# Gated layers with a routed expert matrix: whole-tile copies on ScalarE, the shift on GpSimd, and weight pieces loaded in pairs

## The chip, the cores and the metric

The kernel is one program on one core of a Trainium2 chip (trn2), written directly against the engines: TensorE (PE, and PEld for its weight loads), VectorE (DVE), ScalarE (ACT), GpSimd (POOL) and SyncE (SP), each with its own list of instructions, synchronised by semaphores. The metric is the device time of one execution in microseconds (us). Several executions of the same kernel are timed; their median is compared.

## What is computed

Inputs are `x` (4 x 1024 x 1024, float32), a context `ctx_512` (4 x 1024 x 256), two gate scalars, and the weights of 8 experts (`W`, 8 x 1024 x 1024, with bias and a router `wg`). Cut to what matters:

```python
# layer 1: a rank-one score plane mixed with the normalised x
si, sj = ctx @ Wi, ctx @ Wj                                  # per token
y  = 0.6 * sigmoid(si[:, :, None] + sj[:, None, :] + b) + 0.4 * layernorm(x)
x1 = x + tanh(g_xattn) * y
# layer 2: each token goes to the one expert with the largest logit
xn = layernorm(x1)
logits = xn @ wg ; probs = softmax(logits) ; idx = argmax(probs)
ffn = probs[idx] * (xn @ W[idx].T + b[idx])
out = x1 + tanh(g_ffn) * ffn
```

The 4096 tokens are handled as 32 tiles of 128 tokens (128 partitions x 1024 values).

## The kernel before

**First stage (32 tiles).** SP loads a tile of x into one of 16 buffers (`xr`). DVE takes its statistics (L773, L778). ACT computes the sigmoid as a tanh of a broadcast row plus a per-token bias (`half_tanh`, L592, three tiles ahead) and gets the sum of the tanh over the row as a by-product. From this sum and the mean ACT computes one number per token, the shift `ln_b` (`shift`, L600). POOL applies scale and shift to the tile (`linear`, L475), DVE adds the tanh (`add_tanh`, L784); this also removes the mean of the new row. PE transposes the tile in eight blocks into PSUM (`turn_tile`, L1060). The transposed tile is copied to SBUF in two halves, the lower by ACT (`copy_turned`, L615) and the upper by DVE (L793); PE multiplies it with the router (`route`, L1073). ACT squares the tile and sums (`square`, L606). Every four tiles DVE chooses experts from the logits (`choose`) and computes each token's place in a table (`position`), and POOL stores the rows of a tile, some six tiles behind, by indirect DMA into a table in DRAM sorted by expert (`store`, L483). SP may load tile t + 16 into a buffer only when the rows of tile t have landed in the table (L342). In the same stage eight groups of context are transposed and multiplied by PE (L1032, L1048), up to about tile 17.

**Second stage (up to 42 slots of 128 rows of one expert, here 36 with work).** A loop of 7 turns of 6 slots runs on each engine; every engine reads for each slot from a table whether there is work, and what kind. A slot's rows are loaded twice: as `xb`, in 32 x 32 blocks so that DVE can transpose them (L858), and as `rows` for the result. The transposed rows are cut into a high part (ACT, L668) and a low part (DVE, L862), and PE does 48 matmuls of 128x512 (L1148; high x high, high x low, low x high). DVE finishes the slot (L872), POOL stores it (L537). Each expert's weights, 8 pieces of 128 output rows, are loaded by SP into a ring of 4 piece buffers (`w_raw`), transposed by DVE (L845), and cut by ACT (L662) and DVE (L850) while PE multiplies with the expert before. Pieces 0 to 3 of the next expert are turned in one slot, pieces 4 to 7 in the next.

**The order on SP** in a slot: wait until the rows two slots ahead are transposed, load `xb` three slots ahead (4 DMAs, L281), wait for the output store of the slot before (L380), load `rows` two slots ahead (L285), then the weight pieces that are due: pieces 0 to 3 of the expert after the next one (L387 to L389), or pieces 4 to 7 of the next (L399 to L401). A piece is four DMAs of 128 KB, one for each quarter of the partitions (`load_piece`, L328 to L332), and each waits until the piece that was in its buffer has been transposed. DVE in a slot turns the rows, then the pieces, then finishes the slot.

PE's wait that matters in the second stage is `pe.wait_ge(finished, t + 1)` (L1143): slot t may begin when slot t - 2 has been finished by DVE.

## Time and profile before

| | us |
|---|---|
| median of 3 runs | 660.69 |
| lowest and highest run | 654.01, 662.92 |
| the profiled execution | 661.08 |
| its span, first to last instruction | 659.4 |
| mean granted TensorE clock, share of full speed | 0.922 |

All times within a trace are us from the start of the span. The views of the trace used below are: windows (busy time of each engine in a stretch, with the granted clock and the share and rate of the DMA engines), groups (instructions of one line, engine and operation; after the bar their busy time in us and the mean of one in ns, then the engine's idle time just before them and what ended it), timelines (instructions of one engine in order of time, equal neighbours merged, with the idle time before them in brackets), and the view of one source line. "issue" as an ender is time for which the trace shows nothing that was waited for. SPq is SP's sequencer, which issues DMAs; the number behind it is the time of the issue, not of the transfer.

### The profile page before, as it was taken

What the parts mean: (1) busy time and instruction counts of PE and PEld (TensorE: products, weight loads), DVE (VectorE), ACT (ScalarE), POOL (GpSimd) and SP (SyncE); (2) the same over time, 40 slices, a digit from 0 to 9 for tenths busy, and PEclk for the clock granted to TensorE, in tenths of its full rate; (3) what the DMA queues carried; (4) which work ended last, traced back from release to release, by engine and by line L of the source; (5) the groups of instructions that cost most, each with busy time, mean ns of one, the idle gap of its engine ahead of it and who ended that gap; (6) DMA issues with size and microseconds to landing.
All of it is one profiled execution on the core that took longest, in us unless ns stands there. A gap on an engine that the chain in (4) does not pass through costs nothing.

```text
span 659.4 us, 14149 instructions
## 1 busy us (share of the span) xinstructions
PE 580.0 (88%) x2877; PEld 461.8 (70%) x2878; DVE 424.7 (64%) x558; ACT 277.1 (42%) x440; POOL 309.7 (47%) x465
## 2 busy tenths in 40 slices
PE   8799988887669999998889999986999899899990
PEld 7677766665428878776668877874887688688870
DVE  4578788786789948825853883775378358834420
ACT  4687677575324424413432441433244224422220
POOL 1356666776412364354345335434353364465640
PEclk9699898699798999998889998987999799999995
DMA  7863766784799875866786687476748575656540
GB/s 259 320 222 105 245 231 257 257 257 163 240 284 241 230 229 189 231 181 213 224 236 183 184 231 242 138 226 193 208 149 249 177 222 163 199 159 196 192 132 14
DMA packets 84537, 136.36 MB, mean 207 GB/s; under 512 B 12048, under 2 KB 64784, under 8 KB 84368
## 3 DMA queue, kind: packets, MB, share of 16 engines
q1 hardware_dynamic: 74576, 101.06, 52.1%
q0 software_dynamic: 9792, 33.82, 13.3%
q14 instruction: 157, 1.29, 0.7%
q8 instruction: 12, 0.20, 0.1%
HBM read 101.01 MB, written 35.93 MB: 208 GB/s over the span
## 4 chain that ended last, share of the span: by engine, by line
SPq 23%; issue 21%; PE 19%; DMA 15%; DVE 9%; POOL 6%; ACT 2%; POOLq 1%; ACTq 1%; DVEq 1%
SPq L330 10%; PE pair L1148 10%; DMA out_x<-rows,scatter_row 5%; PE pair L1073 4%; SPq L281 3%; DMA rows<-table 3%; PE pair L1060 3%; SPq L355 3%; DVE wt L850 2%; DVE xr L784 2%; DMA xb<-table 2%; DMA table<-xr,pos 2%; POOL table L483 2%; POOL xr L475 1%; DVE pair L845 1%
## 5 line engine op out<-in xcount | busy, mean ns | idle before, releaser
L1148 PE MATMUL pair<-wt,xt 128*128 x1728 | 415.6, 404 | 34.4 <-DVE rows L872 28.4
L1148 PEld LDWEIGHTS pair<-wt,xt 128*128 128x128 f32 x1728 | 335.7, 195 | 114.4 <-issue 39.6
L525 POOL TENSOR_TENSOR rows<-rows,rb 128x1024 f32<-128x1024 f32 x37 | 88.8, 2400 | 64.6 <-ACT rb L681 63.0
L858 DVE STREAM_TRANSPOSE pair<-xb 128x1024 f32<-128x1024 f32 x38 | 47.8, 1259 | 97.4 <-DMA xb<-table 65.5
L662 ACT ACTIVATE wt<-pair 128x1024 f32 (+1 forms) x64 | 65.6, 1026 | 80.3 <-DVE pair L845 77.9
L668 ACT ACTIVATE xt<-pair 128x1024 fp32r<-128x1024 f32 x38 | 39.0, 1025 | 118.7 <-DVE pair L858 110.6
L845 DVE STREAM_TRANSPOSE pair<-w_raw 128x1024 f32<-128x1024 f32 x64 | 79.8, 1251 | 4.3 <-DMA w_raw<-in_L_ffn_W 1.9
L850 DVE TENSOR_TENSOR wt<-pair,wt 128x1024 f32 (+1 forms) x64 | 77.3, 1208 | 5.9 <-ACT wt L662 5.9
L518 POOL TENSOR_TENSOR scal<-scal,minus_one 128x1 f32<-128x1 f32 x37 | 20.3, 549 | 116.2 <-ACT ez L673 116.2
L681 ACT ACTIVATE rb<-bias_bc,scal 128x1024 f32 (+1 forms) x37 | 46.0, 1244 | 66.1 <-POOL scal L522 66.1
L1073 PE MATMUL pair<-xc_tr,wg_sb 128*8 128x128 f32 x512 | 68.8, 294 | 0.0
L862 DVE TENSOR_TENSOR xt<-pair,xt 128x1024 fp32r<-128x1024 f32 x38 | 46.5, 1223 | 32.9 <-ACT xt L668 28.6
L475 POOL TENSOR_SCALAR xr<-xr,ln_a,ln_b 128x1024 f32<-128x1024 f32 x32 | 45.2, 1414 | 41.4 <-ACT ln_b L600 40.1
L872 DVE SCALAR_TENSOR_TENSOR rows<-pair,scal,rows 128x1024 f32<-128x1024 f32 x36 | 46.1, 1280 | 21.3 <-PE pair L1148 21.3
L1073 PEld LDWEIGHTS pair<-xc_tr,wg_sb 128*8 128x8 f32 x512 | 46.8, 96 | 16.1 <-issue 3.0
L1060 PE MATMUL pair<-ident,xr 128*128 128x128 f32 x256 | 38.3, 297 | 16.4 <-DVE xr L784 16.0
L1060 PEld LDWEIGHTS pair<-ident,xr 128*128 128x128 f32 x256 | 30.9, 153 | 23.5 <-DVE xr L784 21.7
L606 ACT ACTIVATE th<-xr 128x1024 f32<-128x1024 f32 x32 | 33.7, 1052 | 27.6 <-DVE xr L784 27.3
L483 POOL DMA_INDIRECT table<-xr,pos x32 | 35.4, 1105 | 21.0 <-DVE pos L822 11.1
L784 DVE SCALAR_TENSOR_TENSOR xr<-th,c,xr 128x1024 f32<-128x1024 f32 x32 | 42.0, 1312 | 3.4 <-POOL xr L475 3.4
L537 POOL DMA_INDIRECT out_x<-rows,scatter_row x36 | 38.6, 1072 | 11.7 <-issue 6.6
L773 DVE BATCH_NORM_STATS2 raw<-xr 128x6 f32<-128x512 f32 x64 | 40.7, 678 | 3.7 <-DMA xr<-in_x 3.7
(128 smaller groups left out, 384.3 us busy)
## 6 DMA issues: line engine op xcount, KB each, us to landing
w_raw<-in_L_ffn_W SPq DMA_DIRECT2D x256, 128.0 KB
xb<-table SPq DMA_DIRECT2D x156, 128.0 KB
rows<-table SPq DMA_DIRECT2D x38, 520.0 KB, 3.7
xr<-in_x SPq DMA_DIRECT2D x32, 512.0 KB, 6.3
ctx_in<-in_ctx SPq DMA_DIRECT2D x8, 512.0 KB, 5.8
bias_bc<-in_L_ffn_b SPq DMA_DIRECT2D x8, 512.0 KB
sj<-sj_row SPq DMA_DIRECT2D x3, 512.0 KB
out_x<-rows,scatter_row POOLq DMA_INDIRECT x36, 4.6
```

What stands on the lines that cost most here:

```text
L330: sp.dma_start(w_raw[32 * q:32 * (q + 1), m % WR, :, :], in_blocks(W[bass.ds(e, 1), P * m:P * (m + 1), :].rearrange("a o h -> (a o) h"), q ...
L475: nc.gpsimd.tensor_scalar(xr[:, s, 0:H], xr[:, s, 0:H], ln_a[:, t:t + 1], ln_b[:, t:t + 1], ALU.mult, ALU.add).then_inc(lin_ready, 1)
L483: nc.gpsimd.indirect_dma_start(out=table, out_offset=bass.IndirectOffsetOnAxis(ap=pos[:, t:t + 1], axis=0), in_=xr[:, s, :], in_offset=Non ...
L525: nc.gpsimd.tensor_tensor(rows[:, k, 0:H], rows[:, k, 0:H], rb[:, :], ALU.add).then_inc(base_ready, 1)
L662: nc.scalar.activation(wt[:, bass.ds(par, 1), 0, :, P * m:P * (m + 1)].rearrange("p a k o -> p (a k) o"), ps[:, :].rearrange("p (k o) -> p ...
L784: nc.vector.scalar_tensor_tensor(out=xr[:, s, 0:H], in0=th[:, t % RTH, :], scalar=c2[:, 0:1], in1=xr[:, s, 0:H], op0=ALU.mult, op1=ALU.add ...
L845: nc.vector.transpose(turned(ps), blocked(w_raw[:, m % WR, :, :])).then_inc(w_turned, 1)
L850: nc.vector.tensor_tensor(where[:, :, 1].rearrange("p a k o -> p (a k) o"), ps[:, :].rearrange("p (k o) -> p k o", k=K), where[:, :, 0].re ...
L858: nc.vector.transpose(turned(ps), blocked(xb[:, k, :, :])).then_inc(xb_turned, 1)
L1060: last = nc.tensor.transpose(xt_ps[t % 2][:, P * k:P * (k + 1)], xr[:, slot_of(t), P * k:P * (k + 1)], ident[:, :])
L1073: last = nc.tensor.matmul(lgt_ps[:, r, :], wg_sb[:, k, :], xc_tr[:, t % 2, k, :], start=(k == 0), stop=(k == K - 1))
L1148: last = nc.tensor.matmul(out_ps[r % 2][:, HALF * h:HALF * (h + 1)], xt[:, r % RING, x_part, k, :], wt[:, bass.ds(par, 1), w_part, k, HALF ...
```

## The change

1. `shift` moves from ACT to POOL, directly ahead of `linear` of the same tile.
2. The copy of a transposed tile is one instruction of 128x1024 on ACT; DVE's half is gone. PE signals once for all eight blocks.
3. ACT's order within a tile: square of the tile before, copy of this tile, tanh of three tiles ahead (before: tanh of three tiles ahead, square of this tile, copy, shift).
4. Weight pieces load two to a transfer: four DMAs of 256 KB for a pair instead of eight of 128 KB. A pair waits until both pieces in its buffers are transposed, and has one semaphore.
5. POOL looks at the first slot of a turn and, if it has no work, passes the whole turn.

```diff
-            def load_piece(e, m):
+            def load_pieces(e, m):
                 for q in (0, 2, 1, 3):
-                    sp.dma_start(w_raw[32 * q:32 * (q + 1), m % WR, :, :],
-                                 in_blocks(W[bass.ds(e, 1), P * m:P * (m + 1), :].rearrange("a o h -> (a o) h"),
-                                           q)).then_inc(w_landed[m % WR], 16)
+                    sp.dma_start(w_raw[32 * q:32 * (q + 1), m % WR:m % WR + 2, :, :].rearrange("i a b c -> i (a b) c"),
+                                 W[bass.ds(e, 1), P * m:P * (m + 2), QW * q:QW * (q + 1)]
+                                 .rearrange("a (b i) c -> i (a b) c", i=32)).then_inc(w_landed[m % WR // 2], 16)
...
-                                for m in range(WR, K):
-                                    sp.wait_ge(w_turned, K * e + K + m - WR + 1)
-                                    load_piece(e + 1, m)
+                                for m in range(WR, K, 2):
+                                    sp.wait_ge(w_turned, K * e + K + m - WR + 2)
+                                    load_pieces(e + 1, m)
...
+            def shift(t):
+                pool.wait_ge(th_ready, t + 1)
+                pool.wait_ge(ln_ma_ready, t // GR + 1)
+                nc.gpsimd.tensor_scalar(ln_b[:, t:t + 1], xr[:, slot_of(t), TH:TH + 1], nc2h[:, 0:1],
+                                        ln_ma[:, t:t + 1], ALU.mult, ALU.add).then_inc(ln_b_ready, 1)
...
                 if t + 2 < T:
+                    shift(t + 2)
                     linear(t + 2)
...
+                with pool.If(pool.value_load(slot_tab[0:1, 0, bass.ds(TURN * i, 1)], min_val=0, max_val=4) > 0):
+                    slot(TURN * i, 0, i)
+                    for r in range(1, TURN):
...
+                with pool.Else():
+                    pool.nop()
...
-                nc.scalar.activation(xc_tr[:, t % 2, 0:K // 2, :].rearrange("p k n -> p (k n)"),
-                                     xt_ps[t % 2][:, 0:HALF], ACT.Copy).then_inc(xc_copied[0], 1)
+                nc.scalar.activation(xc_tr[:, t % 2, :, :].rearrange("p k n -> p (k n)"), xt_ps[t % 2][:, :],
+                                     ACT.Copy).then_inc(xc_copied, 1)
...
-                if t + RTH - 1 < T:
-                    half_tanh(t + RTH - 1)
-                square(t)
-                copy_turned(t)
-                if t + 2 < T:
-                    shift(t + 2)
+                if t:
+                    square(t - 1)
+                copy_turned(t)
+                if t + RTH - 1 < T:
+                    half_tanh(t + RTH - 1)
...
-            def copy_turned(t):
-                dve.wait_ge(xc_turned[1], t + 1)
...
-                nc.vector.tensor_copy(xc_tr[:, t % 2, K // 2:K, :].rearrange("p k n -> p (k n)"),
-                                      xt_ps[t % 2][:, HALF:2 * HALF]).then_inc(xc_copied[1], 1)
...
-                dve.wait_ge(w_landed[m % WR], 128 * e + 64 * (m // WR) + 64)
+                dve.wait_ge(w_landed[m % WR // 2], 128 * e + 64 * (m // WR) + 64)
```

The program of ACT in the first stage, tile 6 of the kernel before. L592 is the tanh of tile 9, L606 the square of tile 6, L615 the copy of its lower half, L600 the shift of tile 8; the next row begins tile 7.

```order
L592 ACTIVATE th,xr<-sj,si_half 128x1024 [waits xc_ready,mv_ready,sq_ready,si_ready,sj_landed]
L606 ACTIVATE th,xr<-xr 128x1024 [waits xc_ready]
L615 ACTIVATE xc_tr<-pair0 128x512 [waits routed,xc_turned0]
L600 ACTIVATE ln_b<-xr,ln_ma,nc2h 128x1 [waits ln_ma_ready,th_ready]
L592 ACTIVATE th,xr<-sj,si_half 128x1024 [waits xc_ready,mv_ready,sq_ready,si_ready,sj_landed]
```

The same engine and tile in the changed kernel, with its own line numbers: L618 is the square of tile 5, L627 the copy of the whole of tile 6, L611 the tanh of tile 9, and the next row the square of tile 6.

```order
L618 ACTIVATE th,xr<-xr 128x1024 [waits xc_ready]
L627 ACTIVATE xc_tr<-pair 128x1024 [waits routed,xc_turned]
L611 ACTIVATE th,xr<-sj,si_half 128x1024 [waits xc_ready,mv_ready,sq_ready,si_ready,sj_landed]
L618 ACTIVATE th,xr<-xr 128x1024 [waits xc_ready]
L627 ACTIVATE xc_tr<-pair 128x1024 [waits routed,xc_turned]
```

The tanh has moved from ahead of the square to behind the copy, the shift has left the engine, and the copy is twice as wide.

DVE in the first stage, one tile of the kernel before, from the addition to the next one:

```order
L784 SCALAR_TENSOR_TENSOR xr<-th,c,xr 128x1024 [waits lin_ready]
L773 BN_STATS raw<-xr 128x6 [waits x_landed9]
L773 BN_STATS raw<-xr 128x6
L793 COPY xc_tr<-pair 128x512 [waits routed,xc_turned1]
L778 BN_AGGR xr<-raw 128x2 [waits raw_ready]
```

And of the changed kernel:

```order
L794 SCALAR_TENSOR_TENSOR xr<-th,c,xr 128x1024 [waits lin_ready]
L783 BN_STATS raw<-xr 128x6 [waits x_landed9]
L783 BN_STATS raw<-xr 128x6
L788 BN_AGGR xr<-raw 128x2 [waits raw_ready]
L794 SCALAR_TENSOR_TENSOR xr<-th,c,xr 128x1024 [waits lin_ready]
```

The copy and its wait for PE have gone; nothing that DVE waits for within a tile comes from PE any more, save for the choice of experts once in four tiles.

SP in the second stage, the end of a second half in the kernel before (the last piece of an expert; `ISA` rows compute an address):

```order
L400 REGISTER_ALU
L330 ISA [waits w_turned]
L330 DMA w_raw<-in_L_ffn_W 32x4x256
L330 ISA
L330 DMA w_raw<-in_L_ffn_W 32x4x256
...
```

And in the changed kernel (the second pair):

```order
L401 REGISTER_ALU
L331 ISA [waits w_turned]
L331 DMA w_raw<-in_L_ffn_W 32x8x256
L331 ISA
L331 DMA w_raw<-in_L_ffn_W 32x8x256
...
```

Before, this piece of program with one wait and four DMAs stands four times in a half expert, now twice, each DMA with eight blocks of 1 KB for a partition instead of four.

## Rows read from the trace of the kernel before

**Rows 1.** Windows: stretch, length, busy us of each engine, PEclk, DMA share, GB/s.

```profile
42.00:83.00 41.00, 40.36 (x306) 32.20 (x307) 33.83 (x67) 32.32 (x66) 24.45 (x28) 0.88 0.46 157
83.00:166.00 83.00, 67.48 (x527) 52.91 (x528) 63.79 (x124) 54.90 (x113) 57.09 (x61) 0.92 0.66 230
...
198.00:642.00 444.00, 415.55 (x1728) 335.62 (x1728) 276.19 (x265) 154.88 (x205) 204.38 (x327) 0.96 0.68 201
...
230.00:241.00 11.00, 9.42 (x42) 7.43 (x41) 6.96 (x8) 3.48 (x7) 6.54 (x12) 1.00 0.84 264
...
397.00:403.00 6.00, 6.00 (x21) 4.75 (x21) 3.58 (x4) 1.42 (x3) 4.74 (x9) 0.76 0.82 239
```

**Rows 2.** Groups of the first stage, from 83 to 166 us.

```profile
L475 POOL TENSOR_SCALAR xr<-xr,ln_a,ln_b 128x1024 f32<-128x1024 f32 x18 | 26.2, 1454 | 14.4 <-ACT ln_b L600 13.4 <-issue 0.5
...
L1060 PE MATMUL pair<-ident,xr 128*128 128x128 f32 x148 | 22.0, 296 | 15.5 <-DVE xr L784 15.2 <-issue 0.2
...
L773 DVE BATCH_NORM_STATS2 raw<-xr 128x6 f32<-128x512 f32 x25 | 16.0, 680 | 2.3 <-DMA xr<-in_x 2.3
L793 DVE COPY xc_tr<-pair 128x512 f32<-128x512 f32 x18 | 12.4, 689 | 11.3 <-PE pair L1060 10.9 <-issue 0.5
L615 ACT ACTIVATE xc_tr<-pair 128x512 f32<-128x512 f32 x18 | 10.4, 578 | 1.1 <-PE pair L1060 1.0
L600 ACT ACTIVATE ln_b<-xr,ln_ma,nc2h 128x1 f32<-128x1 f32 x17 | 6.4, 375 | 2.4 <-POOL ln_ma L469 2.4
```

**Rows 3.** Groups of the second stage, from 198 to 642 us.

```profile
L1148 PE MATMUL pair<-wt,xt 128*128 x1728 | 415.6, 404 | 34.4 <-DVE rows L872 28.4 <-DVE xt L862 5.9
...
L845 DVE STREAM_TRANSPOSE pair<-w_raw 128x1024 f32<-128x1024 f32 x57 | 71.4, 1253 | 4.3 <-DMA w_raw<-in_L_ffn_W 1.9 <-issue 0.7
L850 DVE TENSOR_TENSOR wt<-pair,wt 128x1024 f32 (+1 forms) x58 | 70.0, 1206 | 3.1 <-ACT wt L662 3.1
...
L858 DVE STREAM_TRANSPOSE pair<-xb 128x1024 f32<-128x1024 f32 x37 | 46.6, 1259 | 96.0 <-DMA xb<-table 64.2 <-issue 31.7 <-DVE xt L862 0.2
```

**Rows 4.** Timeline of PE, slots 7 and 8 together and slot 9.

```profile
281.52 22.61 PE L1148 MATMUL pair<-wt,xt 128*128 x96 [2.71 <-DVE rows L872]
306.55 12.86 PE L1148 MATMUL pair<-wt,xt 128*128 x48 [2.41 <-DVE rows L872]
```

**Rows 5.** Timeline of SP: start, time of the issues, number.

```profile
280.06 9.49 SPq L330 DMA_DIRECT2D w_raw<-in_L_ffn_W  x16
296.03 1.82 SPq L281 DMA_DIRECT2D xb<-table  x4
...
316.73 8.48 SPq L330 DMA_DIRECT2D w_raw<-in_L_ffn_W  x16
```

**Rows 6.** Timeline of DVE in the same stretch.

```profile
287.52 1.26 DVE L858 STREAM_TRANSPOSE pair<-xb 128x1024 f32<-128x1024 f32 x1 [6.41 <-issue]
...
301.25 1.26 DVE L858 STREAM_TRANSPOSE pair<-xb 128x1024 f32<-128x1024 f32 x1 [8.84 <-DMA xb<-table]
...
322.40 1.26 DVE L845 STREAM_TRANSPOSE pair<-w_raw 128x1024 f32<-128x1024 f32 x1
...
325.99 1.26 DVE L845 STREAM_TRANSPOSE pair<-w_raw 128x1024 f32<-128x1024 f32 x1 [1.22 <-DMA w_raw<-in_L_ffn_W]
```

**Rows 7.** Groups with like work: a small one on POOL (stage two), a whole-tile copy on ACT (0 to 30 us).

```profile
L510 POOL TENSOR_SCALAR scal<-rows,c2h,c 128x1 f32<-128x1 f32 x36 | 12.3, 341 | 3.6
...
L565 ACT ACTIVATE xc_tr<-pair 128x1024 f32<-128x1024 f32 x2 | 2.0, 1024 | 0.3 <-PE pair L1032 0.3
```

**Rows 8.** SP's first issues: the timeline, and the source line L300 (ns min/median/max).

```profile
2.24 0.60 SPq L293 DMA_DIRECT2D gates<-in_g_xattn  x1
...
L300 SPq DMA_DIRECT2D xr<-in_x x4: 443/466/3893, 7.0 to 11.9; - x4
```

**Rows 9.** The ends of POOL and SP: durations in ns, first and last start.

```profile
L66 POOLq DRAIN  x1: 5628/5628/5628, 652.7 to 652.7; - x1
...
L66 SPq DRAIN  x1: 13/13/13, 659.2 to 659.2; - x1
```

More of the change, by code:

```diff
@@ L180, in build @@
         row_stored = [sem(f"row_stored{s}") for s in range(RX)]
-        w_landed = [sem(f"w_landed{s}") for s in range(WR)]
+        w_landed = [sem(f"w_landed{s}") for s in range(WR // 2)]
         xb_landed = [sem(f"xb_landed{s}") for s in range(2)]
@@ L213, in build @@
         sq_ready = sem("sq_ready")
-        xc_turned = [sem(f"xc_turned{h}") for h in range(2)]
-        xc_copied = [sem(f"xc_copied{h}") for h in range(2)]
+        xc_turned = sem("xc_turned")
+        xc_copied = sem("xc_copied")
         routed = sem("routed")
@@ L342, in _ @@
                 sp.dma_start(xr[:, slot_of(t), 0:H], tile_of(x_t, t)).then_inc(x_landed[slot_of(t)], 16)
-            for m in range(WR):
-                load_piece(0, m)
-            for m in range(WR, K):
-                sp.wait_ge(w_turned, m - WR + 1)
-                load_piece(0, m)
+            for m in range(0, WR, 2):
+                load_pieces(0, m)
+            for m in range(WR, K, 2):
+                sp.wait_ge(w_turned, m - WR + 2)
+                load_pieces(0, m)
             for s in range(RX):
@@ L360, in _ @@
             load_blocks(sp, row_of(2), 2)
-            for m in range(WR):
-                sp.wait_ge(w_turned, K - WR + m + 1)
-                load_piece(1, m)
+            for m in range(0, WR, 2):
+                sp.wait_ge(w_turned, K - WR + m + 2)
+                load_pieces(1, m)
             with sp.Fori(0, SLOTS // TURN) as i:
@@ L488, in _ @@
             norm_scalars(0)
-            linear(0)
-            linear(1)
+            for t in range(2):
+                shift(t)
+                linear(t)
             for t in range(T):
@@ L529, in _, with slot @@
             pool.wait_ge(limits_told, 1)
[L530 to L543 removed]
+            def slot(t, r, i):
+                slot_scalars(t + 1, 2 * i + (r + 1) // RING, (r + 1) % RING)
+                settled(finished, t + 3)
+                nc.gpsimd.indirect_dma_start(
+                    out=out_rows,
+                    out_offset=bass.IndirectOffsetOnAxis(ap=scatter_row[:, r % RING:r % RING + 1], axis=0),
+                    in_=rows[:, r % RING, 0:H], in_offset=None,
+                    bounds_check=N - 1, oob_is_err=False).then_inc(out_stored[r % RING], 16)
+            with pool.Fori(0, SLOTS // TURN) as i:
+                with pool.If(pool.value_load(slot_tab[0:1, 0, bass.ds(TURN * i, 1)], min_val=0, max_val=4) > 0):
+                    slot(TURN * i, 0, i)
+                    for r in range(1, TURN):
+                        t = TURN * i + r
+                        work = pool.value_load(slot_tab[0:1, 0, bass.ds(t, 1)], min_val=0, max_val=4)
+                        with pool.If(work > 0):
+                            slot(t, r, i)
+                        with pool.Else():
+                            pool.nop()
+                    pool.nop()
+                with pool.Else():
+                    pool.nop()
             held = [pool.value_load(in_place[0:1, s:s + 1], min_val=1, max_val=SLOTS) for s in range(RING)]
@@ L594, in half_tanh @@
                                      accum_out=xr[:, slot_of(t), TH:TH + 1]).then_inc(th_ready, 1)
-            def shift(t):
-                act.wait_ge(th_ready, t + 1)
-                act.wait_ge(ln_ma_ready, t // GR + 1)
-                nc.scalar.activation(ln_b[:, t:t + 1], xr[:, slot_of(t), TH:TH + 1], ACT.Identity,
-                                     bias=ln_ma[:, t:t + 1], scale=nc2h[:, 0:1]).then_inc(ln_b_ready, 1)
             def square(t):
@@ L875, in _ @@
             turn_weights(0, 0, cut_a, 0)
-            for h in range(2):
-                dve.wait_ge(xc_copied[h], T)
+            dve.wait_ge(xc_copied, T)
             turn_weights(0, 1, pair[1], 1)
@@ L1055, in turn_tile @@
                 if t >= 2:
-                    for h in range(2):
-                        pe.wait_ge(xc_copied[h], t - 1)
-                for h in range(2):
-                    for k in range(K // 2 * h, K // 2 * (h + 1)):
-                        last = nc.tensor.transpose(xt_ps[t % 2][:, P * k:P * (k + 1)],
-                                                   xr[:, slot_of(t), P * k:P * (k + 1)], ident[:, :])
-                    last.then_inc(xc_turned[h], 1)
+                    pe.wait_ge(xc_copied, t - 1)
+                for k in range(K):
+                    last = nc.tensor.transpose(xt_ps[t % 2][:, P * k:P * (k + 1)],
+                                               xr[:, slot_of(t), P * k:P * (k + 1)], ident[:, :])
+                last.then_inc(xc_turned, 1)
             def route(t):
-                for h in range(2):
-                    pe.wait_ge(xc_copied[h], t + 1)
+                pe.wait_ge(xc_copied, t + 1)
                 g, r = t // GR, t % GR
```

32 lines of the change are left out of this document (6 added, 26 removed).

## The prediction

> **What bounds the kernel now.** I read the windows of each stage first, then the groups of instructions of one stage at a time with what ended their idle time, and last the timelines of single engines. The windows [rows 1] show three different limits. From 42 to 83 us PE is busy 40.36 of 41 us: nothing that frees another engine can shorten this stretch by more than 0.6 us. From 83 to 166 us it is busy 67.48 of 83. From 198 to 642 us it is busy 415.55 of 444, the last 17 us of the span have no matmul.
>
> In the stretch 83:166 the 18 linear steps (L475) stand for 18 tiles [rows 2], so a tile takes 83/18 = 4.6 us. Busy time per tile is PE 3.75, DVE 63.79/18 = 3.54, POOL 57.09/18 = 3.17, ACT 54.90/18 = 3.05 [rows 1]. No engine is full; what is left is waiting in a ring: PE waited 15.2 us for the addition on DVE, DVE 10.9 us for PE before its half of the copy, POOL 13.4 us for ACT's shift ln_b [rows 2].
>
> In the second stage the reader is to see that PE's idle time ends with DVE's finish of an earlier slot: 28.4 us in sum [rows 3]. DVE in turn spent 64.2 us waiting for the transfer xb, and 1.9 us for weights. A slot of 48 matmuls at full pace is 22.61/2 = 11.3 us; the one behind the pause of 2.41 us takes 12.86 [rows 4]. The granted clock falls in such a place: 0.76 of the full 2.4 GHz on average in 397:403, behind a pause, against 1.00 in 230:241 [rows 1]. 1728/48 = 36 slots of 11.3 are 407 us, so 444 holds 37 us of pauses and slow starts. That is the most that the second part of the change can touch.
>
> Where does xb come late? On SP. The 16 weight transfers that begin at 280.06 take 9.49 us; the next xb loads are issued at 296.03, though the transpose that frees their buffer began at 287.52 and took 1.26 [rows 5, 6]. DVE then stood 8.84 us until 301.25, and PE paused before 306.55 [rows 4, 6]. There are six such groups in the loop, one for the first four pieces of each of the experts 2 to 7.
>
> **First stage, part by part.** DVE loses its copy: 0.689 us a tile and the 10.9 us of waits with it [rows 2]; its busy time falls to 3.54 - 0.69 = 2.85. ACT gets a whole tile instead of a half: a 128x1024 copy out of PSUM took 1.024 against 0.578 [rows 2, 7], so +0.45, and loses the shift, 0.375: 3.05 + 0.07 = 3.12. POOL gets the shift: its own 128x1 tensor_scalar with two scalar columns took 0.341 [rows 7]; with the wait for its own result I take 0.45 (between 0.34 and 0.8), so 3.62. The 13.4 us for which POOL waited on ACT goes, since tanh of a tile is done two tiles ahead. Square one tile behind costs nothing of itself: the store that reads its sum runs six tiles behind, and the tanh that overwrites the same buffer follows it on ACT anyway; were it waited for, it would be 1.24 a tile. ACT's tanh for three tiles ahead now stands behind the copy, which waits for PE; from its end to the addition that needs it there are shift 0.45, linear 1.45, and two tiles of time, so that wait is not expected to be seen.
>
> Next in line are PE with 3.75 and POOL with 3.62 a tile, both close together, so that neither will run without holes. The floor is 3.75: 18 x (4.6 - 3.75) = 15 us, which is PE's wait again. The other end: POOL's collisions, the store-to-load ring (16 buffers; DVE already waited 2.3 us for x [rows 2]), and no gain or +2. I take 4.2 a tile, a bit under the middle: 18 x 0.4 = **-7 us**, range -14 to +2.
>
> **Second stage.** Half as many issues with twice the descriptors. A transfer of 128 descriptors costs SP 9.49/16 = 0.59 us, or 8.48/16 = 0.53 where nothing presses [rows 5]. 256 descriptors in one transfer are not in the trace. The nearest row is the load of 512 single weights (L292): the issue behind it (L293) took 0.60 us. The load of wg, 1024 pieces of 32 bytes, was followed by an issue of 3.89 us (L300, the longest) [rows 8]; a proportional price from it would be 0.97 for 256. So 0.53 to 1.0; I take 0.6, the nearer row. Eight issues are then 4.8 us for 8.5 to 9.5, and SP is at the next xb 4 us sooner. With 1.0 it is no sooner at all.
> The Trainium skill (DMA: Bandwidth & Descriptors, Anatomy of one DMA) says that many descriptors can be emitted before the incremental cost shows up. By it the issue would stay at 0.53 and the gain be near 4.5 us a group; by the wg row it would be nothing. No row here decides between them.
> The bytes do not get fewer. From 230 to 241 us the DMA engines were 0.84 busy at 264 GB/s [rows 1] while 16 pieces' transfers were on their way, and xb now queues behind them. So I count 3.5 us of the 4 for a group. Six groups make 21 us of earlier xb. Of this PE sees what stands before a pause. Some of DVE's long waits the view puts down to issue, not to xb (6.41 us at 287.52) [rows 6], and DVE's own work stays: eight pieces of 1.253 + 1.206 = 19.7 us and twice some 3.7 for the rows and the finish, 27 us, against the 22.6 of two slots on PE [rows 3, 4]. I take 0.6: -13 us.
>
> The other side of the pair: the first piece of a second half can be turned only when its pair has landed. At 316.73 SP begins to issue; DVE turns that first piece at 322.40 and the second at 325.99, after 1.22 us of waiting [rows 5, 6]. Pairs make the first wait for what the second waited for: 0 to 3.6 us, in seven places. The faster issue takes most of it back; I take 0.3 each, +2. SP's wait for turned pieces asks for one piece more, 2.5 us later on DVE. The queue behind it on SP is the rest of the group and the next xb. But where SP begins the second half, at 316.73, DVE's next weight transpose is already the first of that half, so all four of the first are turned [rows 5, 6]: nothing. Sum of the stage **-11 us**, range -22 to +14.
>
> **The stages between and the end.** Between the last tile and the first slot the pieces that share the queue with the last stores are the same bytes: 0, within 1.5 us. In the last turn all six slots are empty. POOL passes one instead of six, but the span does not end with POOL: its drain began at 652.7 and took 5.6, to 658.3, and SP's came last, at 659.2 [rows 9]. SP skips less code now, so what can be had is some 0.9 us: **-1**, range -1 to 0.
> The Trainium skill (Runtime: NRT & Kernel Launch, Instruction fetch mechanics) says that a taken branch out of the fetched window forces a fetch by DMA. DVE's 6.41 us marked issue at 287.52 [rows 6] fit that. By that rule deeper bursts of weights could lengthen such fetches; it is part of the slow rival.
>
> Sum, from the profiled execution's 661.08 (span 659.4, 1.7 around it; the runs' median is 660.69): 661.1 - 7 - 11 - 1 = 642.
>
> **Rivals.**
> A. Issue time goes with descriptors. Then SP is as late as before and stage two gives 0, the pair still costs 2: 661 - 7 + 2 - 1 = 655. For it the wg row; against it the row of 512.
> B. POOL is the new bound of stage one, as the ring of stores and loads holds it at 4.6 a tile; stage two works: 661 - 11 - 1 = 649.
> C. Everything lands: 661 - 14 - 20 - 1 = 626. For it the regular shape of late xb before each pause; against it the DMA share of 0.84 in a group.
> D. Slower: DVE's first piece of each second half waits for its pair. The place is the transpose L845 behind L858 in the seven second-half slots, the price up to 3.6 us each, and as DVE works through there without a pause all of it reaches PE: 25 us. It decides from the point where a pair needs more than the 322.40 - 316.73 = 5.7 us between SP's first issue and DVE's turn. With the first stage's gain 661 + 25 - 7 = 679. Against it: a pair is 1 MB, some 4 us at 264 GB/s.
> E. The change of POOL's turns does nothing because another engine ends last: this is in the forecast already.
>
> **How the numbers follow.** Forecast 0.44 (634 to 648), A 0.21, B 0.16, C 0.13, D 0.06. A measurement tells about 2%, 13 us. Faster than 647.5: most of the forecast's share, C, and a small part of B: 0.58. Within 2%: A, most of B and the rest: 0.37. Slower: 0.05. The range leaves out the far half of C and all of D: 628 to 659.
>
> **What would show it.** Right: in 83:166-like stretches the additions come every 4.2 us, POOL's wait for ln_b is gone, ACT's copy is 1.02; an issue of a double transfer is 0.4 to 0.5 long; xb is issued 3 us or more sooner behind the six groups; DVE's waits for xb fall from 64 to under 50 us and PE's pauses from 28.4 to under 18. Wrong: an issue near 1 us, DVE waiting for w_raw by over 5 us in sum, POOL busy over 90% in the first stage, or PE's pauses as long as before.

## The result, and the profile after

The changed kernel takes 668.84 us (median of 4 runs, 665.38 to 670.98), the kernel before 657.35 (4 runs, 651.73 to 662.92). The ratio is 1.016, with a 95% interval of 1.011 to 1.021: slower by about 11 us, where 642 had been forecast, and outside the range. The profiled execution of the changed kernel took 669.64 us.

The windows of the changed kernel. The columns are those of [rows 1]. The row 189.20:649.10 holds exactly the 1728 matmuls of the second stage, the last row what follows them.

```profile
span 667.8 us, 13667 instructions
...
core 0: us, PE busy (x) PEld busy (x) DVE busy (x) ACT busy (x) POOL busy (x), PEclk, DMA share, GB/s
83.00:166.00 83.00, 67.28 (x554) 52.56 (x552) 55.40 (x116) 60.67 (x100) 64.89 (x78) 0.95 0.76 255
...
189.20:649.10 459.90, 416.70 (x1728) 337.38 (x1728) 276.79 (x265) 154.50 (x205) 205.10 (x328) 0.94 0.74 194
258.00:271.00 13.00, 13.00 (x59) 10.66 (x58) 9.81 (x10) 5.62 (x7) 5.67 (x9) 1.00 1.04 237
649.10:667.80 18.70, 0.01 (x1) 0.00 (x0) 1.28 (x1) 0.00 (x0) 1.07 (x1) 0.60 0.04 11
```

The kernel before, cut at the same places:

```profile
197.90:642.00 444.10, 415.64 (x1728) 335.72 (x1728) 276.29 (x265) 154.88 (x205) 204.38 (x327) 0.96 0.68 201
642.00:659.40 17.40, 0.00 (x1) 0.00 (x0) 1.28 (x1) 0.00 (x0) 1.07 (x1) 0.61 0.04 13
```

So the second stage began 8.7 us sooner, took 15.8 us longer, and what follows it 1.3 us longer: 659.4 - 8.7 + 15.8 + 1.3 = 667.8. Note the DMA share: 0.74 against 0.68 of the engines' time, for a rate of 194 against 201 GB/s. The same bytes keep the DMA engines busy for longer.

The first stage, groups of the window 83:166 (compare [rows 2]):

```profile
L483 POOL TENSOR_SCALAR xr<-xr,ln_a,ln_b 128x1024 f32<-128x1024 f32 x17 | 25.4, 1493 | 1.7
...
L794 DVE SCALAR_TENSOR_TENSOR xr<-th,c,xr 128x1024 f32<-128x1024 f32 x18 | 23.3, 1297 | 5.7 <-POOL xr L483 5.7
L1057 PE MATMUL pair<-ident,xr 128*128 128x128 f32 x144 | 20.2, 284 | 12.5 <-DVE xr L794 12.5
...
L627 ACT ACTIVATE xc_tr<-pair 128x1024 f32<-128x1024 f32 x18 | 18.3, 1018 | 18.7 <-PE pair L1057 18.7
...
L477 POOL TENSOR_SCALAR ln_b<-xr,nc2h,ln_ma 128x1 f32<-128x1 f32 x16 | 7.2, 448 | 2.7 <-ACT th L611 2.2
```

POOL's 13.4 us of waiting for ln_b became 2.7 us ahead of the shift, the copy takes 1.018, and the shift 0.448 where 0.45 was taken. Counting additions in the window misleads, 18 before and 18 after, because the last tile now ends inside it. By the timeline the 18 additions from 84.67 to 155.35 are 17 tiles in 70.7 us, 4.16 a tile; before they were 4.56.

The second stage, what DVE and PE waited for (compare [rows 3]):

```profile
L1144 PE MATMUL pair<-wt,xt 128*128 x1728 | 416.7, 405 | 50.0 <-DVE rows L872 43.2 <-DVE xt L862 6.8
```

```profile
engine line waited for: us in total, times, longest us
DVE pair L858 <- issue: 52.5, 15, 12.7
DVE xt L862 <- ACT xt L678: 39.6, 27, 3.8
DVE rows L872 <- PE pair L1144: 27.3, 7, 5.6
DVE pair L858 <- DMA xb<-table: 25.8, 10, 6.4
DVE pair L845 <- DMA w_raw<-in_L_ffn_W: 16.3, 11, 3.1
```

Waiting for xb fell from 64.2 to 25.8 us, the way that was forecast. But "issue", time for which the profile names no releaser, rose from 31.7 to 52.5, and waiting for weights from 1.9 to 16.3. PE's pauses behind DVE's finish went from 28.4 to 43.2.

SP's timeline (start and length in us), one group of weights, answers to [rows 5], where 16 transfers took 9.49 us:

```profile
277.10 5.50 SPq L331 DMA_DIRECT2D w_raw<-in_L_ffn_W  x8
292.49 1.83 SPq L281 DMA_DIRECT2D xb<-table  x4
```

Issuing is cheap, as forecast: no group of eight in the second stage takes longer than 6.6 us, waits included. But the xb behind this group was issued 15.4 us after its first transfer, for 16.0 us in [rows 5]. The queues and transfers on the page of the changed kernel:

```profile
q1 hardware_dynamic: 72528, 101.05, 57.6%
...
w_raw<-in_L_ffn_W SPq DMA_DIRECT2D x128, 256.0 KB, 6.5
```

The last number is the median time from issue to landing. A group of eight doubles is issued in 3.9 to 6.6 us, but its last byte lands 12 to 16 us after the first issue, no sooner than that of 16 single transfers (11 to 14 us in the first experiment). The xb that SP issued at 264.90, early, landed from 272.7 to 275.2, behind weights of which the last landed at 270.7. DVE turned it only at 291.89, so this late landing alone cost nothing.

### The profile page after: what moved, and what is told of

It is laid out like the page before. It is cut to its first block, busy times and chain, and to the rows that moved or that the text cites. A ratio compares the mean times of both kernels' runs of the same rounds, so it can differ in the third digit from the quotient of the medians.

```text
span 667.8 us, 13667 instructions
## 1 busy us (share of the span) xinstructions
PE 573.7 (86%) x2877; PEld 457.3 (68%) x2878; DVE 403.9 (60%) x526; ACT 280.3 (42%) x408; POOL 326.6 (49%) x497
## 3 DMA queue, kind: packets, MB, share of 16 engines
q0 software_dynamic: 9792, 33.82, 13.3%
## 4 chain that ended last, share of the span: by engine, by line
DMA 25%; issue 19%; PE 19%; POOL 9%; SPq 9%; DVE 9%; ACT 4%; POOLq 1%; ACTq 1%; DVEq 1%
PE pair L1144 10%; DMA out_x<-rows,scatter_row 9%; DMA w_raw<-in_L_ffn_W 8%; PE pair L1069 4%; DVE wt L850 3%; SPq L331 3%; DMA rows<-table 3%; DVE pair L845 3%; POOL table L491 3%; PE pair L1057 2%; DMA table<-xr,pos 2%; ACT rb L691 2%; SPq L281 2%; POOL xr L483 1%; SPq L356 1%
## 5 line engine op out<-in xcount | busy, mean ns | idle before, releaser
L1144 PE MATMUL pair<-wt,xt 128*128 x1728 | 416.7, 405 | 50.0 <-DVE rows L872 43.2
L858 DVE STREAM_TRANSPOSE pair<-xb 128x1024 f32<-128x1024 f32 x38 | 47.8, 1258 | 80.7 <-issue 52.5
L845 DVE STREAM_TRANSPOSE pair<-w_raw 128x1024 f32<-128x1024 f32 x64 | 80.1, 1254 | 19.0 <-DMA w_raw<-in_L_ffn_W 16.3
L1069 PEld LDWEIGHTS pair<-xc_tr,wg_sb 128*8 128x8 f32 x512 | 46.4, 95 | 15.4 <-issue 3.0
L794 DVE SCALAR_TENSOR_TENSOR xr<-th,c,xr 128x1024 f32<-128x1024 f32 x32 | 41.7, 1302 | 13.4 <-POOL xr L483 13.2
L1057 PE MATMUL pair<-ident,xr 128*128 128x128 f32 x256 | 36.4, 287 | 12.5 <-DVE xr L794 12.5
L491 POOL DMA_INDIRECT table<-xr,pos x32 | 37.5, 1171 | 16.5 <-DVE pos L823 6.4
L483 POOL TENSOR_SCALAR xr<-xr,ln_a,ln_b 128x1024 f32<-128x1024 f32 x32 | 43.4, 1356 | 3.2
L627 ACT ACTIVATE xc_tr<-pair 128x1024 f32<-128x1024 f32 x32 | 32.6, 1017 | 26.3 <-PE pair L1057 26.3
L1057 PEld LDWEIGHTS pair<-ident,xr 128*128 128x128 f32 x256 | 29.8, 149 | 18.9 <-DVE xr L794 16.1
## 6 DMA issues: line engine op xcount, KB each, us to landing
bias_bc<-in_L_ffn_b SPq DMA_DIRECT2D x8, 512.0 KB, 10.4
```

The source lines that it names most:

```text
L483: nc.gpsimd.tensor_scalar(xr[:, s, 0:H], xr[:, s, 0:H], ln_a[:, t:t + 1], ln_b[:, t:t + 1], ALU.mult, ALU.add).then_inc(lin_ready, 1)
L491: nc.gpsimd.indirect_dma_start(out=table, out_offset=bass.IndirectOffsetOnAxis(ap=pos[:, t:t + 1], axis=0), in_=xr[:, s, :], in_offset=Non ...
L845: nc.vector.transpose(turned(ps), blocked(w_raw[:, m % WR, :, :])).then_inc(w_turned, 1)
L858: nc.vector.transpose(turned(ps), blocked(xb[:, k, :, :])).then_inc(xb_turned, 1)
L1057: last = nc.tensor.transpose(xt_ps[t % 2][:, P * k:P * (k + 1)], xr[:, slot_of(t), P * k:P * (k + 1)], ident[:, :])
L1069: last = nc.tensor.matmul(lgt_ps[:, r, :], wg_sb[:, k, :], xc_tr[:, t % 2, k, :], start=(k == 0), stop=(k == K - 1))
```

## Experiments

Ratios are to the kernel before, run in turn on the same chip, with their 95% interval. "First slot", "second stage" and "tail" are the start of the 1728 matmuls, their duration, and the rest of the span, of one profiled execution each; they scatter by some 3 us. The intervals are 0.3 to 0.6 points to either side, so a difference of less than some 0.7 points between two of these ratios is not told apart from noise.

**1. Single pieces again, all else changed** (four transfers of 128 KB with a semaphore and a wait of their own; the other calls alike).

```diff
-                for m in range(0, WR, 2):
-                    load_pieces(e + 2, m)
+                for m in range(WR):
+                    load_piece(e + 2, m)
```

> The changed kernel with its weight pieces loaded one by one again (128 KB transfers, one semaphore and one wait per piece), all else as changed. Theory (the loss is in the paired loads alone): the first slot begins near 189 us as in the changed kernel (before: 197.9), the second stage is back at 444 us instead of 460, and the time is 1.2 to 1.5% below the kernel before, about 649 of 657. DVE waits for weight pieces under 4 us in sum (16.3 in the changed kernel). Rival (the early start of the second stage, or a change elsewhere, spoils its order): the second stage stays over 452 us and the time is at or above the kernel before.

Ratio 0.998 (0.994 to 1.002). First slot 194.5, second stage 445.5, tail 18.9. The loss is in the paired loads, as the theory says; DVE's wait for weights was 2.7 us. But the rest of the change wins almost nothing, where 1.2 to 1.5% was expected.

**2. The kernel before with paired loads alone** (part 4 of the diff, nothing else).

> The kernel before with the paired loads alone. Theory (pairs cost the second stage 16 us by themselves): the first slot begins near 198 us, the second stage takes about 460 us, the time is 2.0 to 2.7% above the kernel before. Rival (the pairs hurt only together with the other parts, as what precedes them has moved): within 1% of the kernel before.

Ratio 1.017 (1.012 to 1.022), first slot 200.8, second stage 457.4. Pairs cost the same by themselves, if a little less than the 2.0 to 2.7% expected. The rival is out.

**3. The pair's wait with 128 KB transfers.**

```diff
-                for q in (0, 2, 1, 3):
-                    sp.dma_start(w_raw[32 * q:32 * (q + 1), m % WR:m % WR + 2, ...
+                for n in (m, m + 1):
+                    for q in (0, 2, 1, 3):
+                        sp.dma_start(w_raw[32 * q:32 * (q + 1), n % WR, ...
```

> The changed kernel, but a pair goes out as eight transfers of 128 KB in the order of the kernel before; the pair's wait on SP and its single semaphore stay. Theory 1 (the price is the wait: the first piece of a pair is turned only when both have landed): as slow as the changed kernel, ratio 1.01 to 1.02, DVE waits for weight pieces over 14 us. Theory 2 (the price is the form of the transfers: twice as long in one quarter of the partitions, at 218 GB/s, and issued in a denser burst): close to the kernel with single pieces, ratio 0.985 to 0.995, waits of DVE for weights under 8 us. Between them: both have a share.

Ratio 0.990 (0.985 to 0.994), second stage 442.1. The wait for the pair costs nothing; the form of the transfers is the loss, 2.6% between this kernel and the changed one. DVE waits for weights 10.4 us, where under 8 was expected, and the kernel is none the slower for it. DVE's waits:

```profile
DVE pair L859 <- issue: 44.0, 14, 9.1
DVE pair L859 <- DMA xb<-table: 38.9, 14, 6.1
DVE xt L863 <- ACT xt L679: 30.3, 25, 2.6
DVE rows L873 <- PE pair L1145: 22.0, 5, 5.6
DVE pair L846 <- DMA w_raw<-in_L_ffn_W: 10.4, 7, 2.3
```

**4. Single pieces, quarters in the order 0, 1, 2, 3** (experiment 1 with another order, nothing else).

> The kernel with single pieces (as the first of these runs), but the four transfers of a piece go to the quarters of the partitions in the order 0, 1, 2, 3 instead of 0, 2, 1, 3, so that two in a row lie in the same half of the partitions, 256 KB as in a double transfer. Theory (the double transfers are slow because both halves' ports are not in use together): the rate in a group of pieces falls from about 260 towards 220 GB/s and the second stage becomes 5 to 15 us longer than with 0, 2, 1, 3. Rival (it is the wait, or the denser issue): the time is within 0.5% of the kernel with single pieces in the order 0, 2, 1, 3.

Ratio 0.996 (0.992 to 0.999). Both are half right: the bytes move more slowly, but here it cost no time. The first pair of rows is of experiment 1, the second of this one:

```profile
q1 hardware_dynamic: 74576, 101.06, 52.2%
...
w_raw<-in_L_ffn_W SPq DMA_DIRECT2D x256, 128.0 KB, 3.3
```

```profile
q1 hardware_dynamic: 74576, 101.06, 56.4%
...
w_raw<-in_L_ffn_W SPq DMA_DIRECT2D x256, 128.0 KB, 3.9
```

Times the spans (658.9 and 652.0), the 101 MB took 344 us of the 16 engines' time in one order and 368 in the other; the doubles took 385.

**5. Doubles with a pause between them**, in the loop alone (`paced` is set there).

```diff
                                 .rearrange("a (b i) c -> i (a b) c", i=32)).then_inc(w_landed[m % WR // 2], 16)
+                    if paced:
+                        sp.value_load(slot_tab[0:1, 0, 0:1], min_val=0, max_val=4)
```

> The changed kernel with its double transfers, but in the loop SP reads one register value (about 0.6 us) behind each of them, so that 256 KB are issued every 1.1 us, as densely as the single pieces were. Theory (the dense burst is what hurts: it fills the queue ahead of xb and of the other transfers): the time comes back to near the kernel with 128 KB transfers and the pair's wait, ratio 0.99 to 1.00. Rival (the size of a transfer and the speed at which it moves is what hurts, however it is spaced): ratio 1.01 to 1.02 as the changed kernel, or worse by the delay.

Ratio 1.010 (1.004 to 1.016). Eight issues took 7.9 to 10.0 us, 16 single ones 7.6 to 9.8 in experiment 1. It lies at the lower end of what the rival expected. Spacing takes back 0.6 of 2.6 points at most, and that is within the noise.

**6. All engines pass an empty turn**, on top of experiment 3; SP, ACT, PE and DVE get what the change gave POOL:

```diff
             with dve.Fori(0, SLOTS // TURN) as i:
+                with dve.If(dve.value_load(slot_tab[0:1, 0, bass.ds(TURN * i, 1)], min_val=0, max_val=4) > 0):
                     for r in range(TURN):
...
+                with dve.Else():
+                    dve.nop()
```

> The kernel with the pair's wait and 128 KB transfers, and SP, ACT, PE and DVE also pass a whole turn when its first slot is empty, as POOL does. Theory (the end is set by DVE and SP, which step through six empty slots at 1.5 to 2.6 us each behind the last matmul): the tail behind the last matmul falls from 18.7 us to 9 to 12, and the time by 6 to 9 us against the same kernel without it, ratio to the kernel before 0.975 to 0.982. Rival (the last transfers or the fetch of the code behind the loop set the end): tail over 16 us, no gain.

Ratio 0.989 (0.984 to 0.995), where 0.975 to 0.982 was expected. The tail did what was expected:

```profile
190.20:639.30 449.10, 413.37 (x1728) 334.76 (x1728) 276.22 (x265) 154.56 (x205) 204.53 (x327) 0.96 0.67 199
639.30:652.10 12.80, 0.00 (x0) 0.00 (x0) 1.28 (x1) 0.00 (x0) 1.07 (x1) 0.64 0.03 11
```

12.8 us instead of 18.7: behind the last matmul it was DVE and SP that stepped through six empty slots. In this execution DVE was done 4.7 us behind the last matmul and POOL's drain came last. In the changed kernel, where only POOL passed the turn, POOL's drain could begin at 6.8 us but DVE came to its own at 18.4. The second stage was 7 us longer than in experiment 3, and ate the gain. Why is open; the code of every engine has moved.

**7. The first stage's edits alone** (parts 1 to 3 on the kernel before).

> The kernel before with the first stage's three edits alone (shift on GpSimd, whole copy on ScalarE, square one tile behind); single pieces, and GpSimd steps through every slot. Theory (they win what the trace showed, 8 to 9 us, and the rest of the kernel keeps its time): ratio 0.985 to 0.990. Rival (the win is partly given back in the second stage, because DVE's program has moved and its taken branches fetch code more often: 33 fetches over 0.35 us instead of 28 in the kernels with these edits): ratio 0.993 to 1.000 and a second stage longer than 444 us.

```profile
188.30:634.30 446.00, 410.85 (x1728) 332.54 (x1728) 276.38 (x265) 154.40 (x205) 204.59 (x327) 0.96 0.68 201
634.30:652.70 18.40, 0.00 (x0) 0.00 (x0) 1.28 (x1) 0.00 (x0) 1.07 (x1) 0.63 0.04 13
```

Ratio 0.999 (0.996 to 1.002): the rival. The first slot begins at 188.3, almost 10 us sooner, but the stage is 2 us and the tail 1 us longer, and the profiled execution was a quick one (654.4 to 662.9, median 658.3).

**8. Doubles in one half of an expert only.** In 8a pieces 0 to 3 go as doubles and 4 to 7 as in experiment 3; in 8b it is the other way round.

> Doubles of 256 KB only for pieces 0 to 3 of each expert (loaded one expert ahead); pieces 4 to 7 go as eight transfers of 128 KB per pair. Theory (the loss is DVE's wait for the second halves, which it turns as soon as they land): most of the loss is gone, ratio 0.990 to 1.000. Rival (the loss is in the first halves, whose burst stands ahead of the next xb): ratio 1.008 or more.

> Doubles only for pieces 4 to 7, 128 KB transfers for pieces 0 to 3. Theory (loss in the second halves): ratio 1.008 or more. Rival (loss in the first halves): 0.990 to 1.000. If both of this pair of kernels lie in the middle, each half has a share.

Ratios 0.999 (0.994 to 1.004) and 1.016 (1.009 to 1.022), against 0.990 without doubles and 1.016 with both. Most of the loss is in the second halves, which DVE turns as soon as they are there. The first halves cost something too, if alone; the two do not add. The runs of 8a scatter more than others, from 652.7 to 669.2 us.

**9. A loop body of 12 slots instead of 6**, on top of experiment 6.

```diff
-    TURN = 2 * RING
+    TURN = 4 * RING
```

(The counts of the output stores per turn follow, and two small tables share their memory with others, to fit.)

> The kernel in which all engines pass an empty turn, with the loop's body 12 slots long instead of 6, so that DVE jumps back to the loop's start three times and not six while there is work. Theory (a jump back costs DVE 3 to 8 us, since its code is fetched through a DMA queue behind the weights, and PE pauses for it): DVE's gaps behind branches fall by 8 to 12 us in sum, PE's pauses behind slots 5/6/7, 18 to 20 and 30 shrink or go, the second stage shortens by 5 to 12 us; ratio 0.97 to 0.985. Rival (the gap is the burst itself: DVE would wait for xb or weights instead): second stage within 3 us of the same kernel with 6.

Ratio 0.984 (0.980 to 0.989), the fastest of all kernels here, 650.7 us. DVE's waits:

```profile
DVE pair L867 <- DMA xb<-table: 49.3, 12, 10.1
...
DVE pair L867 <- issue: 22.8, 13, 8.8
```

"Issue" fell from 45.3 us in experiment 6 to 22.8, and PE's pause ahead of slot 20, behind the former jump at slot 18, from 6.47 us to 3.40. Part of it came back as waiting for xb, and the stage of this execution is 446.9: the stage is 2.2 us shorter than in experiment 6, which is what the rival expected (within 3 us), while the ratio is in the theory's range. The gain of half a per cent over experiment 6 is within the noise.

**10. The changed kernel with a body of 12 slots and nothing else.**

> The changed kernel (double transfers) with a loop body of 12 slots and nothing else. Theory (over half of what the doubles cost is the longer fetch of code at jumps back, 27 us in sum against 19 before): ratio 0.99 to 1.005 and DVE's gaps behind branches fall from 65 to about 50 us. Rival (the doubles cost by late landings of xb and weights): ratio stays over 1.01.

```profile
192.70:644.50 451.80, 414.95 (x1728) 334.63 (x1728) 276.85 (x265) 154.51 (x205) 204.55 (x327) 0.95 0.75 198
644.50:679.20 34.70, 0.00 (x0) 0.00 (x0) 1.28 (x1) 0.00 (x0) 1.07 (x1) 0.57 0.05 14
```

Ratio 1.029 (1.025 to 1.033), a miss. The second stage shortened by 8.1 us, but with 48 slots 12 are empty behind the end, and the tail grew by 16 us. I had left that out. Experiment 14 repeats it without the tail.

**11. The kernel before with the pair's wait, 128 KB transfers.**

> The kernel before with the pair's wait and single semaphore, transfers still 128 KB. Theory (the pair's wait itself costs nothing, or wins a little, since SP stands in fewer waits within a group): ratio 0.992 to 1.002. Rival (the first piece of a pair that waits for the second costs 5 us or more, and the changed first stage only hid it): ratio 1.006 or more.

Ratio 0.996 (0.992 to 0.999). With experiment 2 it makes a clean pair: same waits, and the same code save for SP's issues; only the transfers differ. DVE's waits of this one, then of experiment 2:

```profile
DVE pair L860 <- DMA xb<-table: 54.5, 16, 11.2
DVE pair L860 <- issue: 34.1, 14, 9.5
DVE xt L864 <- ACT xt L670: 29.7, 25, 2.1
DVE rows L874 <- PE pair L1150: 14.5, 3, 5.6
DVE pair L847 <- DMA w_raw<-in_L_ffn_W: 13.3, 9, 3.3
```

```profile
DVE pair L859 <- issue: 45.8, 14, 12.1
DVE pair L859 <- DMA xb<-table: 34.0, 10, 8.5
DVE xt L863 <- ACT xt L669: 30.7, 27, 2.4
DVE rows L873 <- PE pair L1149: 29.1, 7, 6.1
DVE pair L846 <- DMA w_raw<-in_L_ffn_W: 16.4, 11, 3.1
```

**12. Experiment 3 in the order 0, 1, 2, 3.**

> The kernel with the pair's wait and 128 KB transfers (ratio 0.990), but the quarters in the order 0, 1, 2, 3. Theory 1 (bytes that move more slowly are what doubles cost): the weights' queue takes a share near 56 to 57% as with doubles, and the ratio rises to 1.00 to 1.01. Theory 2 (what counts is how many bytes stand in the queue at once, and those are spaced by 0.5 us per 128 KB here): the share rises too, but the ratio stays at 0.988 to 0.996.

Ratio 0.998 (0.994 to 1.001), second stage 445.3, q1 at 55.7% for 53.8%. It falls between the two: slower bytes cost 0.8 points here, just over the noise, and none in experiment 4.

**13. Doubles for all experts but the first.**

> The changed kernel, but expert 0's eight pieces, loaded while the first stage ends, go in 128 KB transfers; all others stay doubles. Theory (doubles also slow the last tiles' loads and stores: the first slot began at 193.8 us on average in five runs with them against 189.8 in six without): first slot near 190 us, ratio 1.008 to 1.014 against 1.016 for the changed kernel. Rival (that difference is scatter of single profiles): ratio 1.015 to 1.02.

Ratio 1.015 (1.011 to 1.018), first slot 189.8. The ratio is at the rival's edge (1.015 to 1.02) and not clear of the theory's (1.008 to 1.014), and the first slot is where the theory put it, in one execution. So what is loaded during the first stage costs at most a small part; more these runs do not tell.

**14. Doubles, body of 12 slots, empty turn passed by all engines.**

> The changed kernel with a loop body of 12 slots and an empty turn passed by all engines: the run with 12 slots and doubles had a tail of 34.7 us, 19 more than with passing. Theory: tail 13 to 16 us, second stage near 452 us, ratio 0.998 to 1.006, so that doubles still cost 1.3 to 2% against the same kernel with 128 KB transfers (0.984), and rarer jumps have taken back some 1%. Rival (jumps are no part of it): ratio over 1.008.

```profile
188.80:639.20 450.40, 416.06 (x1728) 337.18 (x1728) 276.65 (x265) 154.51 (x205) 204.62 (x327) 0.95 0.75 199
639.20:654.20 15.00, 0.00 (x0) 0.00 (x0) 1.28 (x1) 0.00 (x0) 1.07 (x1) 0.67 0.04 11
```

Ratio 1.003 (1.000 to 1.006), as expected. Doubles cost 1.9 points against experiment 9, and 2.6 with bodies of 6 slots: 0.7 points may hang on the jumps, but that difference is within the noise.

## Why the prediction was wrong

**The first stage** was right in its mechanism and its size: 4.16 us a tile for a forecast 4.2, DVE freed, POOL's wait gone, and the second stage starting 8.7 us sooner for 7 forecast. (What holds a tile over PE's 3.75 us is in part a thing the prediction only touched: DVE waited 8.7 us for x in this window, for 2.3 before.) What failed is the silent step behind it, that a sooner start is a sooner end. Alone, the edits moved the time by -0.1% (experiment 7). In five kernels with these edits, 128 KB transfers and bodies of 6 slots (1, 3, 4, 7, 12) the first slot began at 190.1 on average, against 197.4 in the two with neither these edits nor doubles (before and 11). Their second stages took 445.1 on average against 443.5, and their tails 18.7 against 17.0: 3.4 of the 7.2 us come back. DVE's gaps behind branches that are longer than 0.35 us number 28 in the second stage of before and 11 each, with a sum of 38 and 39 us, and 34 in each of the five, with a sum of 45 to 49 us. That this is a matter of where the moved code lies is argued, not shown.

**The second stage** has the wrong sign: +15.8 for -11. The step that failed is the value of an xb issued sooner, "So I count 3.5 us of the 4 for a group" and then "I take 0.6: -13 us". In four of the six groups xb was issued 3.5 to 4.7 us sooner behind the group's first transfer, but it had to land behind the same weights, whose last byte came no sooner: its own last byte came 14.6 to 15.8 us after that first transfer, for 15.5 to 16.2 in experiment 3. The prediction had priced this queue at 0.5 us a group. In the other two, the prediction's own example among them, it was issued only 0.6 us sooner. There SP's loop jumps back between the weights and xb. SP's sequencer shows a gap of 3.4 us behind that jump at 291.0 in the kernel before, part of the 16 us between 280.06 and 296.03, which the prediction had put down to the issues. In the changed kernel the gap is 7.1 us (at 283.8) and 7.2 us (at 518.6), and takes back what the issues saved. The prediction also named the wrong transpose for that xb: the one that frees its buffer had ended at 267.6, and the one at 287.52 frees the next.

The waits for xb did fall by 38 us, but what DVE does not spend on xb it spends on other things that come by DMA. In the changed kernel DVE never waits for PE from 184.2, just ahead of the first slot, to 457.6, when slot 20 begins: 273.4 us for the stretch that took 259.9 in experiment 3 and 259.7 before. So DVE's waits in it count in full. Summed from DVE's timeline over this stretch:

| us | changed | experiment 3 | experiment 2 | experiment 11 |
|---|---|---|---|---|
| length of the stretch | 273.4 | 259.9 | 269.9 | 259.5 |
| ahead of rows' transpose, issue | 32.5 | 27.0 | 27.0 | 20.6 |
| same, xb | 23.2 | 23.5 | 27.7 | 29.4 |
| waiting for ACT's high part | 17.7 | 12.2 | 13.7 | 10.7 |
| waiting for weights | 9.3 | 6.8 | 10.5 | 8.6 |

The last two columns are the clean pair: of 10.4 us, issue is 6.4, ACT 3.0, weights 1.9, and xb gives back 1.7. These are single executions.

**What "issue" is here** can be read at one place. DVE's timeline at the end of the third turn, changed kernel:

```profile
430.65 1.28 DVE L872 SCALAR_TENSOR_TENSOR rows<-pair,scal,rows 128x1024 f32<-128x1024 f32 x1
440.59 1.26 DVE L858 STREAM_TRANSPOSE pair<-xb 128x1024 f32<-128x1024 f32 x1 [8.65 <-issue]
441.76 1.22 DVE L845 STREAM_TRANSPOSE pair<-w_raw 128x1024 f32<-128x1024 f32 x1
445.04 1.23 DVE L862 TENSOR_TENSOR xt<-pair,xt 128x1024 fp32r<-128x1024 f32 x1 [2.06 <-ACT xt L678]
```

and in experiment 3:

```profile
421.46 1.28 DVE L873 SCALAR_TENSOR_TENSOR rows<-pair,scal,rows 128x1024 f32<-128x1024 f32 x1
429.20 1.26 DVE L859 STREAM_TRANSPOSE pair<-xb 128x1024 f32<-128x1024 f32 x1 [6.46 <-issue]
```

The xb of this slot had landed at 422.95, long before. DVE's sequencer shows the branch that closes the loop at 431.24, and its next instruction at 439.54. SP had begun a group of eight doubles at 428.26, the last of which landed at 441.57. In experiment 3 the same jump took 5.3 us, in the kernel before 3.9. Then, in the changed kernel, at 442.98, the third instruction could have run, but ACT, itself late from a jump of 5.8 us, was 2.06 us behind. Over the second stage DVE's gaps behind branches sum to 65.7 us in the changed kernel, 54.9 in experiment 2, and 39.3 in 11.

Experiment 8 shows that the doubles lengthen the jumps. At the end of the first and the fourth turn SP has just issued a first half, at the end of the third a second half. The gaps behind the jump back, in us:

| | transfers of the first halves, the second halves | DVE, turns 1, 3, 4 | SP, turns 1, 3, 4 |
|---|---|---|---|
| before | single, single | 3.6, 3.9, 4.4 | 3.4, 4.9, 3.4 |
| experiment 3 | single, single | 4.5, 5.3, 4.4 | 2.9, 4.4, 2.6 |
| changed | double, double | 6.5, 8.3, 5.9 | 7.1, 8.1, 7.2 |
| 8a | double, single | 8.7, 4.6, 5.5 | 7.4, 3.9, 6.9 |
| 8b | single, double | 3.7, 8.4, 4.4 | 2.6, 7.9, 2.6 |
| 5, doubles with a pause | double, double | 6.7, 4.8, 5.1 | 3.0, 5.4, 2.6 |

Each is one execution. In all kernels here with bodies of 6 slots SP's jump took 6.0 to 8.1 us behind doubles without a pause, and 2.6 to 5.4 behind other transfers.

The prediction had this in one sentence with no price. The Trainium skill (Runtime: NRT & Kernel Launch, Instruction fetch mechanics) says that a taken branch out of the fetched window forces a fetch by DMA before execution goes on; the packets of q14 in such gaps agree with it. Experiment 9 agrees in part: with two jumps back in the second stage instead of five, "issue" halved, but most of it came back as other waits.

**The transfers themselves.** A double stays in one quarter of the partitions for 256 KB. Experiments 4 and 12 make single transfers do nearly the same, two in a row in one half, and q1's time goes from 344 to 368 us and from 350 to 365, towards the doubles' 385. The doubles issued from 257.94 to 261.71 landed one every 1.26 us (261.9 to 270.7), 209 GB/s; the window around it shows 237 GB/s with all queues at a share of 1.04, for 264 at 0.84 in [rows 1]. The Trainium skill (SBUF — State Buffer, Door 1: The DMA port swizzle) says that 64 partitions reach no more ports than 32 do, half of the 16, with some 218 GB/s as the limit for large transfers; the order's effect and this group's 209 agree with that, but no run here shows that the ports are the cause. I had not looked at which partitions a transfer fills.

**How the 2.6 points divide** is open. That the form of the transfers costs them is shown (2 against 11, changed against 3). Spacing the issues took back 0.6 (5), rarer jumps 0.7 (14 against 9), both within the noise; slower bytes alone cost 0.8 or nothing (12, 4); these overlap. Longer jumps alone do not explain the loss: DVE's gaps behind branches sum to 67.7 us in 8a and 51.4 in 8b, yet 8a is the faster one, by some 1.6 points. That second halves cost most (8b) fits the stretch where DVE is the bottleneck, but no run shows which of its waits it is.

**The pair's wait**, my rival D and the +2 in the sum: nothing. DVE waits 13.3 instead of 1.9 us for weights in experiment 11, yet the ratio is 0.996; its waits for xb are 54.5 instead of 64.2. What D gave as its sign did appear: the pair issued from 257.94 had landed at 265.63, 7.7 us later and not some 4, and DVE waited 16.3 us for weights in sum. In experiments 3 and 11, at 10.4 and 13.3 us, such waits cost nothing. **The tail**: +1.3 for -1. That POOL's passing would do nothing was right; that the end would follow SP was not: DVE steps through the empty slots too, and came last. **Rival A** did not come true: the issue of a double has the same median as that of a single transfer, 0.317 us. The place in the Trainium skill that the prediction cites for this (DMA: Bandwidth & Descriptors, Anatomy of one DMA) is about transfers that GpSimd issues; what SP's cost, these rows show.

## What to carry to other kernels

Before merging transfers to save issue time, ask what stands behind them: if the queue is busy, an earlier issue only waits longer. Look also at what the issuing engine does between its transfers: here a jump back to its loop's start took 7 to 8 us behind a burst of doubles, for 3 to 5, and ate the saving. Time marked "issue" behind a loop's end is a cost of its own; longer loop bodies and passing empty turns on every engine, together with the pair's wait on 128 KB transfers, made the fastest kernel here (experiment 9, 0.984), though what each of them is worth is within the noise, and other waits took the place of much of it. And a stage that starts sooner is worth only what the end shows: measure the part alone.

## What was not expected of the hardware

- One order of quarters against another (0, 2, 1, 3 or 0, 1, 2, 3), same bytes, same sizes: 344 or 368 us of DMA engine time.
- A jump back to a loop's start costs DVE 3.3 to 4.4 us in the kernel before, and 5.9 to 8.3 in the changed kernel where doubles were issued just ahead of it; SP 3.4 to 4.9 us and 7.1 to 8.1. Each empty slot stepped through costs DVE 2.4 to 2.8 us with nothing to do.
- Taking an instruction out of DVE's first stage went with more gaps behind its branches in the second: 28 became 34.
